# A decoder layer on one core: smaller temperature groups, a thinner self-attention step, later preparations, and constant products added to the steps with little work

## The reference, cut to what matters

```python
x = x + self_attention(layernorm(x))          # 16 heads of 8 channels, rotary, causal, out @ Wo + bo
x = x + cross_attention(layernorm(x), ctx)    # 16 heads, 77 keys
x = x + experts(layernorm(x))                 # 8 experts, top 2, low-rank, F = 512

# inside the cross-attention, per sequence and head:
scores = (Q @ K.T) / sqrt(8)
feats  = [scores.mean(), scores.max(-1).mean(), softmax(scores).var(-1, ddof=1).mean()]
hidden = gelu(w1 @ feats + b1); hidden = gelu(w2 @ hidden + b2)      # 64 wide, exact gelu
t      = exp(clip(w3 @ hidden + b3, log 0.1, log 10))
attn   = softmax(Q @ K.T / (2 t))
out    = attn @ V;  result = out @ Wo + bo
```

## Time and profile before

| | us |
|---|---|
| runs, median of 3 | 1848.47 |
| profiled execution, its own time | 1853.18 |
| its span | 1851.4 |
| TensorE busy in the span | 1695.9 (92%) |
| VectorE, ScalarE, GpSimd busy | 1238.7, 921.6, 848.8 |
| mean granted TensorE clock | 0.913 of full |

### The profile page before, as it was taken

How to read it: one execution, slowest core, us unless ns; L and a number is a source line. 1 busy time by engine, 2 the same in 40 slices (tenths; PEclk the granted TensorE clock), 3 DMA queues, 4 the chain that set the end, 5 groups by cost and what they waited for, 6 DMA issues and landing times. The chain is left out here.

```text
span 1851.4 us, 42638 instructions
## 1 busy us (share of the span) xinstructions
PE 1695.9 (92%) x14420; PEld 1267.3 (68%) x14420; DVE 1238.7 (67%) x2792; ACT 921.6 (50%) x2143; POOL 848.8 (46%) x892
## 2 busy tenths in 40 slices
PE   0999999999976799999999999886899999999998
PEld 0455555555544566666666666543899999999998
DVE  4666666666655656777777777312777787778776
ACT  1455555555542345666666665433554545454543
POOL 0433444443325556777667776320343344334432
PEclk9999999999985558999999999655899999999999
DMA  5000000000000000000000000000000000000000
GB/s 161 2 2 1 1 1 1 1 1 1 1 6 6 5 4 6 7 7 7 7 6 8 6 7 4 2 2 1 4 7 9 9 9 6 9 9 9 6 9 13
DMA packets 26311, 16.50 MB, mean 9 GB/s; under 512 B 6179, under 2 KB 23525, under 8 KB 26213
## 3 DMA queue, kind: packets, MB, share of 16 engines
q1 hardware_dynamic: 26212, 15.23, 2.9%
HBM read 9.97 MB, written 4.19 MB: 8 GB/s over the span
## 5 line engine op out<-in xcount | busy, mean ns | idle before, releaser
L836 ACT ACTIVATE xa_P<-xa_SK 77x1024 f32<-77x1024 f32 x128 | 130.6, 1020 | 161.8 <-PE xa_SK L1116 161.8
L283 ACT ACTIVATE sa_P<-sa_SK 128x1024 f32<-128x1024 f32 x128 | 131.2, 1025 | 147.2 <-PE sa_SK L426 147.2
L249 POOL TENSOR_TENSOR sa_KM<-sa_HQK,sc_headmask 128x512 fp32r<-128x512 f32 x64 | 66.5, 1039 | 292.1 <-ACT sa_HQK L278 292.1
L1394 POOL TENSOR_TENSOR ff_zz<-ff_zt 128x256 f32<-128x256 f32 x32 | 38.4, 1199 | 319.8 <-DVE ff_zt L1591 319.8
L1462 ACT ACTIVATE ff_SG<-bank 128x512 f32<-128x512 f32 x128 | 76.8, 600 | 192.0 <-PE bank L1664 191.8
L1581 DVE TENSOR_TENSOR ff_GL<-ff_GU,ff_GH 128x512 fp32r<-128x512 f32 x128 | 147.4, 1171 | 27.5 <-ACT ff_GH L1467 27.2
L356 DVE TENSOR_REDUCE sa_mx<-sa_SQ 128x8 f32<-128x1024 f32 x128 | 156.5, 1223 | 6.8 <-PE sa_SQ L426 5.4
L770 POOL TENSOR_TENSOR xa_QMH<-xa_QBH,xc_headmask 128x512 fp32r<-128x512 f32 x64 | 72.7, 1136 | 190.8 <-ACT xa_QBH L826 190.8
L1729 PE MATMUL bank<-fh_r,ff_GH 128*128 128x256 f32 x512 | 148.4, 290 | 0.0
L1662 PE MATMUL bank<-ff_ZH,fh_b 128*128 128x256 f32 x512 | 147.7, 289 | 0.0
L1663 PE MATMUL bank<-ff_ZL,fh_b 128*128 128x256 f32 x512 | 145.1, 283 | 0.0
(11 more groups left out here) (257 smaller groups left out, 5444.1 us busy)
## 6 DMA issues: line engine op xcount, KB each, us to landing
xa_shift<-xa_row SPq DMA_DIRECT2D x256, 2.0 KB
out<-X SPq DMA_DIRECT2D x64, 64.0 KB, 1.5
xa_cx<-ctx SPq DMA_DIRECT2D x64, 38.5 KB
sa_shift<-sa_mT SPq DMA_DIRECT2D x64, 8.0 KB, 1.8
fr_b<-L_ffn_B SPq DMA_DIRECT2D x2, 256.0 KB, 3.9
fr_r<-down_a SPq DMA_DIRECT2D x1, 512.0 KB, 4.7
fr_w<-L_ffn_w_gate SPq DMA_DIRECT2D x1, 256.0 KB, 3.5
fr_w<-L_ffn_w_up SPq DMA_DIRECT2D x1, 256.0 KB, 3.6
```

The costliest lines, as they stand in the source:

```text
L283: nc.scalar.activation(P[:, 2 * (k % 2) + h, :], SK[:], ACT.Exp).then_inc(p_ready, 1)
L836: nc.scalar.activation(P[0:TC, (2 * b + h) % 4, :], SK[0:TC, :], ACT.Exp).then_inc(p_ready, 1)
```

## The change

Self-attention:
- `pv` packs two heads into 32 rows, so that O has two blocks of 128 columns in place of four; `o_copy` copies 256 columns, `o_transpose` turns two tiles, `norm` reads them with other strides.
- The product ones times bo is gone. bo is loaded as 128 equal rows, and GpSimd adds it to X one step before the step's `norm` (`add_bias`, a 128x128 addition); VectorE's residual waits for it.

Cross-attention:
- GROUP is 4 in place of 8, in a ring of 4 groups (16 slots as before); the small network works on 64 columns in place of 128 and has 16 rounds, at n = 5, 9, ... 65. LAG is 7. Scores only in steps 0 to 6, both in 7 to 63, outputs only in 64 to 73.
- The fills: TensorE waits only for two small ones at the start. VA is filled in two parts (ahead, and at n = 0), P in quarters (n = 1 to 4), HK's and LK's pads at n = 2 and 3 (the pads only), shift at n = 4; the small network's weights at n = 0, the bias at n = 2; heads at n = -2, pick at n = 1.
- The maxima's transpose and `mlp3` stand inside `by_key(.., 1)`, behind its first two pairs of products, and no longer ahead of it.
- `filler`: products of two constant tiles, pick times heads (128x512), into banks that no one reads at that time. In steps 2 to 6 four ahead of the scores (into SK) and six ahead of the maxima's transpose (SK); in steps from 64 on six ahead of `o_transpose` (SQ), but for the step with a round.

The diff, cut to its core:

```diff
@@ self_attention @@
+            def add_bias(b):
+                pool.wait_ge(xn_ready, b + 1)
+                xb = X[:, bass.ts(b, C)]
+                nc.gpsimd.tensor_tensor(xb, xb, bo_rows[:], ALU.add).then_inc(biased, 1)
...
-                nc.scalar.copy(o[:], O[:]).then_inc(o_sb, 1)
+                nc.scalar.copy(o[:], O[:, 0:2 * T]).then_inc(o_sb, 1)
...
                 dve.wait_ge(proj_ps, b + 1)
+                dve.wait_ge(biased, b + 1)
...
-                for g in range(QUADS):
-                    last = tr(R[:, g * T:(g + 1) * T], o[:, g * T:(g + 1) * T], ident[:])
+                for h in range(2):
+                    last = tr(R[:, h * T:(h + 1) * T], o[:, h * T:(h + 1) * T], ident[:])
...
-                mm(L[:, T:T + C], ones_row[:], bo[:], start=True, stop=False)
-                mm(L[:, T:T + C], onT[:], wo[:], start=False, stop=True).then_inc(proj_ps, 1)
+                mm(L[:, T:T + C], onT[:], wo[:], start=True, stop=True).then_inc(proj_ps, 1)
@@ cross_attention @@
-    GROUP = 8
-    SLOTS = 2 * GROUP
+    GROUP = 4
+    RINGS = 4
+    SLOTS = RINGS * GROUP
-    LAG = 11
+    LAG = GROUP + 3
-    VRING = 15
+    VRING = 12
+    HIDDEN = slice(3 * T, 3 * T + GROUP * H)
+    FIRST = 4
...
+                if n == 0:
+                    values(FIRST, VRING, 2)
+                if 1 <= n <= 4:
+                    nc.gpsimd.memset(P[:, n - 1], 0.0).then_inc(p_set, 1)
...
+                if n == 0:
+                    prepare()
+                if n == 2:
+                    split_bias()
+                    nc.vector.memset(HK[:, :, TC:T].bitcast(F32), 0.0).then_inc(pads_set, 1)
+                if n == 3:
+                    nc.vector.memset(LK[:, :, TC:T].bitcast(F32), 0.0).then_inc(pads_set, 1)
+                if n == 4:
+                    nc.vector.memset(shift[:].bitcast(F32), 0.0).then_inc(shift_set, 1)
...
-            def by_key(b, h):
+            def by_key(b, h, between=None):
...
+                    if part == 0 and between is not None:
+                        between()
...
+            def filler(where, count):
+                for _ in range(count):
+                    mm(where, pick[:, 0], heads[:, 0:512], start=True, stop=True)
...
-            pe.wait_ge(const_set, 4)
-            pe.wait_ge(pads, PADS)
-            pe.wait_ge(act_set, 2)
+            pe.wait_ge(ones_set, 2)
...
             for n in STEPS:
                 r = mlp_round(n)
+                if n == 2:
+                    pe.wait_ge(pick_set, 1)
+                if n == B:
+                    pe.wait_ge(e1_ready, B)
                 if real(n - LAG - 2):
                     project(n - LAG - 2)
+                if 2 <= n < LAG:
+                    filler(SK[:, 0:512], 4)
...
                 elif real(n - LAG - 1):
+                    if n >= B:
+                        filler(SQ[:, 0:512], 6)
                     o_transpose(n - LAG - 1, r)
...
                 if real(n - LAG):
-                    by_key(n - LAG, 1)
+                    by_key(n - LAG, 1, maxima)
+                else:
+                    if 2 <= n < LAG:
+                        filler(SK[:, 512:1024], 6)
+                    maxima()
```

More of the change, by code:

```diff
@@ L472, in pv @@
                     need(pe, o_sb, b)
[L473 to L478, removed]
+                for e in range(2):
+                    for t in range(4):
+                        head = 2 * t + e
+                        at = 256 * e + 32 * (4 * h + t)
+                        last = mm(O[32 * t:32 * t + 32, h * T:h * T + T], VA[:, k].rearrange("k e x -> k (e x)")[:, at:at + 32],
+                                  P[:, 2 * (k % 2) + h, head * T:head * T + T], start=(h == 0 and e == 0), stop=(e == 1),
+                                  skip_group_check=True)
                 last.then_inc(pv_ps, 1)
@@ L604, in cross_attention @@
         onT = sb("onT", [C, T])
-        const_set = sem("const_set")
-        act_set = sem("act_set")
-        pads = sem("pads")
+        ones_set = sem("ones_set")
+        mT_set = sem("mT_set")
+        va_set = sem("va_set")
+        p_set = sem("p_set")
+        pads_set = sem("pads_set")
+        shift_set = sem("shift_set")
+        heads_set = sem("heads_set")
+        pick_set = sem("pick_set")
         prepared = sem("prepared")
@@ L750, in low @@
             def low(b):
-                need(pool, pads, PADS)
                 pool.wait_ge(h_ready, 2 * b + 2)
@@ L862, in _ @@
             rows4 = ident[:].rearrange("k (g r) -> k g r", r=32)[:, :, 0:1]
-            nc.scalar.copy(pick[:], rows4.to_broadcast([128, QUADS, T])).then_inc(act_set, 1)
-            nc.scalar.copy(heads[:].rearrange("h (g k) -> h g k", k=TC),
-                           ident[:, 0:H].unsqueeze(2).to_broadcast([128, H, TC])).then_inc(act_set, 1)
-            act.wait_ge(const_set, 4)
-            act.wait_ge(pads, PADS)
-            act.wait_ge(prepared, PREPARED)
-            act.wait_ge(bias_ps, 1)
-            nc.scalar.copy(bias_high[:], R[0:2, 0:C]).then_inc(bias_sb, 1)
             for n in STEPS:
@@ L897, in _ @@
                     exp_e(n)
+                if n == -2:
+                    nc.scalar.copy(heads[:].rearrange("h (g k) -> h g k", k=TC),
+                                   ident[:, 0:H].unsqueeze(2).to_broadcast([128, H, TC])).then_inc(heads_set, 1)
+                if n == 1:
+                    nc.scalar.copy(pick[:], rows4.to_broadcast([128, QUADS, T])).then_inc(pick_set, 1)
+                    act.wait_ge(bias_ps, 1)
+                    nc.scalar.copy(bias_high[:], R[0:2, 0:C]).then_inc(bias_sb, 1)
         @block.vector
@@ L963, in factors @@
             def factors(r):
[L964 removed]
+                part = slice(r % RINGS * GROUP, r % RINGS * GROUP + GROUP)
                 dve.wait_ge(mlp_act, 3 * r + 3)
[L966 removed]
+                need(dve, row_sb, GROUP * (r - RINGS + 1))
                 nc.vector.tensor_scalar(CF[:], CF[:], math.exp(-LOG_T_MAX), None, ALU.max).then_inc(clipped, 1)
@@ L1161, in mlp1 @@
                 need(pe, onT_sb, n - LAG - 1)
+                if r == 0:
+                    pe.wait_ge(prepared, PREPARED + 1)
                 for f in range(3):
-                    last = mm(R[0:64, 3 * T:4 * T], w1s[:, f, :], of_group(FEAT[:, f], r), start=(f == 0), stop=(f == 2))
+                    last = mm(R[0:64, HIDDEN], w1s[:, f, :], of_group(FEAT[:, f], r), start=(f == 0), stop=(f == 2))
                 last.then_inc(mlp_ps, 1)
```

141 lines of the change are left out of this document (78 added, 63 removed).

## The result

The changed kernel takes 1771.81 us (median of 4 runs, 1767.61 to 1772.35) against 1852.47 in the runs of before beside it; the ratio is 0.9558 with a 95% interval of 0.9523 to 0.9593. Forecast were 1766, 1744 to 1815. The profiled execution took 1771.94 with a span of 1770.1, so 81.3 less in the span.

The account below looks back on a forecast made before the run. TensorE was taken to set the pace, busy in the middle, at half clock at both ends of the cross-attention. Terms -34, -9.4, +2.2, +5.4, +4, -51 sum to -82.8: 1853.2 to 1770.4 profiled, 1766 median, range 1744 to 1815.

Parts of the forecast that it names:

- Self-attention, -34: Self-attention: two transposes (0.245) and the bias product (0.26) save 0.51 in 63 steps, plus 2 for the drain: -34 us.
- Start, steps 0 and 1, steps 2 to 6: -9.4, +2.2, +5.4: Cross-attention's beginning: earlier first product -9.4, fills in steps 0 and 1 +2.2, constant products in scores-only steps +5.4 us.
- Steps 7 to 63, +4: Full cross-attention steps: 57 of 8.72, 14 rounds of 2.7 and 8 for clock dips, 543 against 538.84: +4 us.
- about cancel: Rounds: products on 64 columns and the later maxima cancel, leaving 2.7 a round over a step of 8.72.
- The tail, -51: Output-only steps: ten in place of 14, with constant products, 65 us against 116.10: -51 us.
- The step that failed: First full steps of the cross-attention: they begin at full clock, where three at 14.48 were 17 us over.
- constant products don't raise the clock: Rival, both ends of the cross-attention: clock stays low, +12, +17 and +24, about 1819 us; chance 0.10.
- falls at the rounds eat the gain: Rival, full steps: the clock falls at every round and does not come back, slower, up to 1928 us; chance 0.07.
- the milder form: Rival, full steps: three rounds lose two steps each to the clock, +35, 1801 us; chance 0.15.
- the self-attention gains the transposes only: Rival, self-attention: qkv then waits for xnT, so -16 for -34, 1784 us; chance 0.13.
- the middle is held up: Rival, full steps: ScalarE delays by_key's second half and the later maxima's transpose costs 0.2 a step, +18, 1784; chance 0.10.

Follow-up runs that it names:

- a3: The changed kernel without the constant products of the scores-only steps, keeping those of the output-only steps: 1770.43 us, ratio 0.9560.
- b1: The kernel before with the changed self-attention alone (two transposes for four, bias added by GpSimd): 1825.02 us, ratio 0.9852.
- a4: The changed kernel with as many constant products, of the same length, on 32 rows in place of 128: 1811.91 us, ratio 0.9762.
- b4: The changed kernel with groups of 8, two rings, a lag of 11 and 15 slots of V: 1765.23 us, ratio 0.9534.
- b3: The changed kernel with the maxima's transpose ahead of by_key's second half again: 1814.92 us, ratio 0.9771.
- a1: The changed kernel without any of its constant products: 1792.31 us, ratio 0.9660.
- b2: The kernel before with only the packing of two heads in 32 rows, the bias product kept: 1838.06 us, ratio 0.9916.
- d1: b3 with three full-height constant products added in each round: 1782.72 us, ratio 0.9569.
- c1: The changed kernel with three more full-height constant products in each of the 16 rounds: 1761.73 us, ratio 0.9544.
- a2: The changed kernel without the constant products of the output-only steps, keeping those of the scores-only steps: 1781.48 us, ratio 0.9608.
- c3: b4 with products in the rounds and at the self-attention's start, and fillers from step 1 with heads in place of pick: 1755.09 us, ratio 0.9463.

## Why the prediction was right, point by point, and where it was not

**Self-attention, -34.** Measured -25.2 in the profile, in two parts. The step is 7.15, not 7.08: the two transposes gave 0.20 in place of 0.245 and the bias product 0.24 in place of 0.26, which is 4 us. The other 5 lie at the start of the stage. In the profile of before the first products by key are short already, in that of the changed kernel they are at half clock. The timelines, before and then after:

```profile
56.87 0.82 PE L445 MATMUL sa_SK<-sa_shift,sa_pick_row 128*128 128x512 f32 x2
```

```profile
59.40 1.41 PE L457 MATMUL sa_SK<-sa_shift,sa_pick_row 128*128 128x512 f32 x2
```

In a3 and b1, whose self-attention is the same as the changed kernel's, they come at 57 and the cross-attention starts at 520.4 and 520.3. Of the ten profiles with this self-attention, the first rise to 1.00 is at 50 to 51 us in four (a3, a4, b1, b4; start of the cross-attention 520.0 to 520.6), at 62.0 in b3 (523.4), at 66.5 to 68.8 in four more, the changed kernel's the latest of them (525.1 to 525.9), and at 73.1 in a1 (528.2). So the removed products are worth 30.8 where the rise is early, and the moment of the rise moves the end by 5 to 8 us. Before had it at 50.5 and b2 at 56.4; one profile of each does not show whether the change has a part in late rises. A term read from one execution carries that much.

**Start, steps 0 and 1, steps 2 to 6: -9.4, +2.2, +5.4.** Measured -10.2, +2.4, +4.0. The first product stands at 528.19, 2.3 after the stage's start, where I took 2.4.

**Steps 7 to 63, +4.** Measured +1.6, by terms that were all off. A plain step is 8.58, not 8.72: ScalarE did not bind, it had idle time left ahead of the exponential. The timeline of a step of the changed kernel:

```profile
685.27 1.02 ACT L865 ACTIVATE xa_P<-xa_SK 77x1024 f32<-77x1024 f32 x1 [1.05 <-PE xa_SK L1157]
...
689.22 0.28 PE L1131 MATMUL xa_O<-xc_ident,xa_FEAT 128*16 128x128 f32 x1
689.42 0.49 PE L1157 MATMUL xa_SK<-xa_QML,xa_HK 32*128 32x512 f32 x2
```

L1131 no longer waits for the maxima, had 0.56 there. Against that, a round costs 37.20 less 4 x 8.58, so 2.9 in place of 2.7, and the falls of the clock took 12.5 in place of 8. In a round the prediction let the products on 64 columns and the later maxima "about cancel". They do not: a round in the old place (d1) costs 37.40 less 4 x 8.83, so 2.1, and in the new one (c1) 37.44 less 4 x 8.60, so 3.0, three products included in both. The move costs about 1.0 in each round and gives 0.23 in each step, which with groups of four is nothing at full clock; the prediction gave it 0.12 a step. So the small error of this term is luck: the clock, which made the new place pay (b3), was not in the sum for it.

**The tail, -51.** Measured -53.9: four steps fewer at 10.04 are 40, and the constant products are 14 (a1, a2). A step is 7.12 where 7.3 was forecast, and the round's step takes 11.7 and the next 10.8, forecast 11.5 and 10.5.

**The step that failed** is the claim that full steps begin at full clock thanks to the fillers of the scores-only steps, and that this saved three steps of 14.48, 17 us. a3 has no such fillers and the same time, and a1 has none and lost 5 there in its profile. The place of the maxima's transpose decides far more: b3 and d1 have the fillers and the old place, and take 55.80 and 51.30 for the first four full steps; d1 differs from c1 (36.00) in nothing else. The start of the cross-attention, -10.2 by later fills, has no experiment of its own.

**The rivals.** That constant products don't raise the clock: refuted in the changed kernel (steps 2 to 6 at 0.79 with them, 0.50 without), and a4, where they are 32 rows high, is that rival made true: 1812, for which I had worked out 1819, and "about 1826" before the run. Its scores-only steps (59.50 for 59) and its tail (+25.6 for +24) came as worked out; the first full steps lost 9, not 17. Its tail step is 11.89, not 11.7, since a step had 0.93 idle and not 1.2. That falls at the rounds eat the gain: ten of the 14 rounds had one, 12.5 us together, and two of them outlasted the round's step, so the milder form held in part; with the transpose in its old place (b3) about half of the gain is gone. That the self-attention gains the transposes only is refuted by b2 (7.39, and 7.15 without the bias product), and that the middle is held up by the plain step of 8.58.

## What to carry to other kernels

Look at the granted clock stage by stage before counting instructions; where it is 0.50 beside a busy TensorE, ask how many rows of the array its products use. A few full-height products of constants into a free bank, in the time in which TensorE waits anyway, can pay for themselves (14 us in this tail); of small height they only cost (20 us, a4 against a1). Where a stage comes to full clock by itself, they give little or nothing (a3). And split a change that gains before believing in its parts: here the smaller groups gave nothing that the runs can tell and the first fillers far less than the 17 forecast, and the sum still fit to 1.5 us. A stage read from one execution can be off by 5 us or more when the clock rises in it.

## What was not expected of the hardware

- Moving the maxima's transpose by four products (in a round the network's third product with it) changed the time by about 40 us, through the clock (b3), though at full clock it is worth nothing over a group (37.40 and 37.44).
- Three products, 0.94 us at full clock in the timeline of c1, in each round: the clock stayed at 1.00 over 530 us of full steps in which it had fallen ten times. The profiles of c3 and d1 show no fall behind these rounds either, once the clock is up, for 475 and 491 us.
- TensorE busy 11.89 of 11.89 us a step stayed at 0.50 for the whole tail when the added products were 32 rows high, and the same products at 128 rows brought 1.00.
- Runs of d1 differ by 30 us, and the longer they are the lower is their mean clock: 1766, 1778, 1788 and 1797 at 0.971, 0.963, 0.956 and 0.952. The profiles of b1 and of the changed kernel, with the same self-attention, start the cross-attention 5.6 apart, with the first rise of the clock at 50.6 and 68.8.
